# Second attention of a two-layer kernel: who splits, copies and divides the small rows between the big matmuls

## The reference, cut to what matters

```
x_norm = _rms_norm(x, g)
q = (x_norm @ w_q) ... * rf          # 16 heads of width 8
k = (x_norm @ w_k) ... * rf          # 4 heads
v = x_norm @ w_v
qkt  = einsum('brkqa,bkca->brkqc', q5, k) / sqrt(128)
attn = softmax(qkt, axis=-1)         # exp(s - rowmax(s)) / sum
s    = einsum('brkqc,bkca->brkqa', attn, v)
o    = s @ w_o
return s + o
```

## Time and profile before

| what | value |
|---|---|
| span of the profiled execution | 1651.9 us |
| second attention in it | about 520 to 1450 us |
| one batch of it (o in the middle) | 53.40 us |
| busy: PE matmuls / PE weight loads | 1455.9 (88%) / 716.9 (43%) us |
| busy: DVE / ACT / POOL | 1180.7 (71%) / 946.4 (57%) / 833.9 (50%) us |
| largest groups | `row_max` L1592 649.8 us on DVE, `exps` L1496 567.1 us on ACT, `scores` L1798 347.7 us on PE |

### The profile page before, as it was taken

How to read it: one execution, slowest core, us unless ns; L and a number is a source line. 1 busy time by engine, 2 the same in 40 slices (tenths; PEclk the granted TensorE clock), 3 DMA queues, 4 the chain that set the end, 5 groups by cost and what they waited for, 6 DMA issues and landing times. The chain is left out here.

```text
span 1651.9 us, 30013 instructions
## 1 busy us (share of the span) xinstructions
PE 1455.9 (88%) x9488; PEld 716.9 (43%) x9488; DVE 1180.7 (71%) x3123; ACT 946.4 (57%) x1805; POOL 833.9 (50%) x941
## 2 busy tenths in 40 slices
PE   3999999969993279999999999999999999849996
PEld 1444444469993123333333333333333332239996
DVE  3688777833334568899889998899989998514443
ACT  2565556524441147777777778777777777612221
POOL 4688888743003463556555655556565620114443
PEclk9999999979997569999999999999999999969998
DMA  1111211289995111122112221122212210347771
GB/s 38 46 56 54 64 56 49 80 242 298 304 296 145 57 56 46 56 77 73 55 55 65 78 61 54 57 75 73 59 55 62 70 51 13 108 155 239 236 241 58
DMA packets 144965, 165.76 MB, mean 100 GB/s; under 512 B 29073, under 2 KB 115217, under 8 KB 142649
## 3 DMA queue, kind: packets, MB, share of 16 engines
q1 hardware_dynamic: 92377, 74.76, 15.2%
q10 hardware_dynamic: 38608, 58.62, 11.6%
q0 software_dynamic: 13824, 30.47, 6.0%
HBM read 111.93 MB, written 51.30 MB: 99 GB/s over the span
## 5 line engine op out<-in xcount | busy, mean ns | idle before, releaser
L1592 DVE TENSOR_REDUCE c_mx<-c_ps_mx 128x1 f32<-128x512 f32 x1024 | 649.8, 683 | 89.6 <-PE c_ps_mx L1828 82.1
L1496 ACT ACTIVATE c_pt<-c_ps_e 128x512 f32<-128x512 f32 x1024 | 567.1, 601 | 189.9 <-PE c_ps_e L1798 176.3
L1798 PE MATMUL c_ps_e<-c_qst,c_kex 74*128 74x512 bf16 (+1 forms) x1024 | 347.7, 388 | 3.5 <-ACT c_pt L1496 1.9
L1811 PE MATMUL c_ps_v<-c_pt,c_vp 128*32 128x512 f32 x2048 | 274.5, 608 | 1.1 <-ACT c_pt L1496 0.7
L1333 POOL DMA_INDIRECT c_gy<-ys,mt x128 | 124.2, 970 | 276.5 <-PE c_ps_v L1811 129.9
L1828 PE MATMUL c_ps_mx<-c_kex,c_qst 64*128 64x512 bf16 x1024 | 204.6, 396 | 57.9 <-DVE c_mx L1592 40.9
L1828 PEld LDWEIGHTS c_ps_mx<-c_kex,c_qst 64*128 64x128 bf16 x1024 | 49.3, 93 | 367.8 <-DVE c_mx L1592 345.3
L998 PE MATMUL f_ps_h<-f_xT,f_w 128*128 128x256 f32 x800 | 197.0, 386 | 0.2 <-DVE f_xT L1064 0.2
L558 ACT ACTIVATE a_pt<-a_ps_s,temp 128x1024 f32<-128x1024 f32 (+3 forms) x128 | 113.1, 884 | 91.3 <-PE a_ps_s L652 86.3
L499 POOL DMA_INDIRECT xs<-a_xn,a_meta x128 | 135.6, 1059 | 38.1 <-issue 35.3
L998 PEld LDWEIGHTS f_ps_h<-f_xT,f_w 128*128 128x128 f32 x800 | 145.4, 194 | 15.9 <-issue 0.6
(11 more groups left out here) (225 smaller groups left out, 1895.0 us busy)
## 6 DMA issues: line engine op xcount, KB each, us to landing
f_w<-in_we ACTq DMA_DIRECT2D x80, 321.0 KB, 4.4
f_w<-in_we ACTq DMA_DIRECT2D x37, 576.0 KB, 4.5
c_qst<-qparts SPq DMA_DIRECT2D x75, 192.0 KB
f_x<-rows SPq DMA_DIRECT2D x40, 257.0 KB, 3.9
f_x<-xs SPq DMA_DIRECT2D x80, 128.0 KB, 4.4
ys<-f_y ACTq DMA_DIRECT2D x80, 128.0 KB, 4.3
qparts<-c_qp SPq DMA_DIRECT2D x16, 384.0 KB, 2.5
x<-in_x SPq DMA_DIRECT2D x16, 256.0 KB, 3.0
```

The costliest lines, as they stand in the source:

```text
L1496: nc.scalar.activation(pt[:, s % 4, hl, :], ps_e[:, e_bank(64 * b + n)], ACT.Exp, scale=QSCALE).then_inc(exp_done, 1)
L1592: nc.vector.tensor_reduce(mx[:, g % 2, col:col + 1], ps_mx[:, m_bank(64 * b + 2 * m + par)], AX, ALU.max).then_inc(mx_done, 1)
L1798: nc.tensor.matmul(ps_e[:, e_bank(64 * b + n)], kex[rows, p, k_head(hl), kt * P:(kt + 1) * P], qst[rows, p, q_head(g, hl), :], start=True, ...
L1811: last = nc.tensor.matmul(ps_v[32 * hl:32 * (hl + 1), :], vp[:, p, kt, hl, :], pt[:, s % 4, hl, :], start=kt == 0, stop=kt == NT - 1)
```

## The change

**Shift rows.** Before, PE transposed the 16 columns of maxima (float32), and DVE negated them and split them into two bfloat16 parts with two instructions out of PSUM. Now POOL splits the columns in SBUF (`split`: a cast to bfloat16, a wait for it, and a subtraction, 128x16 each, into `c_mxp`), PE turns both parts with one bfloat16 matmul (32 rows), and ACT negates and copies them to `c_shb`. SP's four DMAs stay; only their source's layout is new. PE's `max_columns` waits for `split_ready` and no longer for `mx_done`.

**Result rows.** Before, DVE took the reciprocal of the sums and multiplied, out of PSUM, four times a batch. Now ACT copies the 36 used columns of each of 4 blocks (`token_copy`, to `c_raw`) four times a batch, DVE takes one reciprocal of all 64 sums (`inverses`), and POOL multiplies once (`normalise`, 128x512). `s_rows` waits for POOL (`all_ready`).

**Places.** The small blocks are in other steps. PE: `s_rows` 2 to 3, `s_project` 3 to 4, `max_columns` of group 2 from 4 to 5, `token_rows` of group 0 from 5 to 6, `x_rows` from the middle of 7 to the end of 7, and the first `project` from the end of 7 to the middle of 8. `output` moves from step 4 to 5 on DVE; `xT_copy` and the first `prj_copy` from step 7 to 8 on ACT. On POOL the scatters carry the steps 6 to 9 instead of 5 to 8.

```diff
@@ POOL
+                def normalise(i, o):
+                    pool.wait_ge(rcp_ready, b + 1)
+                    pool.wait_ge(sT_ps, b)
+                    nc.gpsimd.tensor_tensor(sall[...], raw[...][:, :, 0:DH1], rcp[...].to_broadcast([P, NT * H1, DH1]),
+                                            ALU.mult).then_inc(all_ready, 1)
+                def split(i, o, g):
+                    pool.wait_ge(mx_done, 16 * (4 * b + g + 1) + 2)
+                    if not (isinstance(b, int) and 4 * b + g < 2):
+                        pool.wait_ge(mt_ps, 4 * b + g - 1)
+                    nc.gpsimd.tensor_copy(mxp[:, g % 2, 0], mx[:, g % 2]).then_inc(split_steps, 1)
+                    pool.wait_ge(split_steps, 4 * b + g + 1)
+                    nc.gpsimd.tensor_tensor(mxp[:, g % 2, 1], mx[:, g % 2], mxp[:, g % 2, 0], ALU.subtract).then_inc(split_ready, 1)
                 def body(i, o):
+                    split(i, o, 1)
                     if nxt2:
                         combine(ln, i, o + 2)
                     if nxt:
                         v_rows(i, o + 1)
+                    if prev:
+                        normalise(i, o - 1)
                     keep_xn(i, o)
                     if nxt2:
                         norms(ln, i, o + 2)
+                    split(i, o, 2)
+                    if nxt2:
                         normal_rows(i, o + 2)
                     if prev:
-                        for t in range(NT):
-                            scatter(i, o - 1, t, 5 + t)
+                        for t in range(3):
+                            scatter(i, o - 1, t, 6 + t)
+                    split(i, o, 3)
+                    if prev:
+                        scatter(i, o - 1, 3, 9)
...
                         gather(i, o + 3, (1,), 11)
                         gather(i, o + 3, (2,), 12)
+                    if nxt:
+                        split(i, o + 1, 0)
                     if nxt2:
                         k_parts(pc, i, o + 2)
@@ ACT
                     for s in range(16):
                         exps(i, o, s, 0)
-                        if s == 7 and nxt2:
+                        if s == 2 and prev:
+                            token_copy(i, o - 1, 3)
+                        if s in (7, 11, 15):
+                            token_copy(i, o, s // 4 - 1)
+                        if s in (1, 6, 9):
+                            shifts(i, o, s // 4 + 1)
+                        if s == 13 and nxt:
+                            shifts(i, o + 1, 0)
+                        if s == 8 and nxt2:
                             xT_copy(i, o + 2)
...
-                        if s == 2 and prev:
+                        if s == 3 and prev:
                             sT_copy(i, o - 1)
-                        if s == 7 and nxt2:
+                        if s == 8 and nxt2:
                             prj_copy(i, o + 2, 0)
@@ DVE
-                        if s in (1, 5, 9):
-                            shifts(i, o, s // 4 + 1)
-                        if s == 13 and nxt:
-                            shifts(i, o + 1, 0)
-                        if s == 1 and prev:
-                            normalise(i, o - 1, 3)
+                        if s == 2 and prev:
+                            inverses(i, o - 1)
-                        if s in (5, 10, 14):
-                            normalise(i, o, s // 5 - 1 if s < 14 else 2)
@@ PE
-                    pe.wait_ge(mx_done, 16 * (4 * b + g + 1) + 2)
-                    nc.tensor.transpose(ps_j[:, 0:P], mx[:, g % 2, :], k.ident[:]).then_inc(mt_ps, 1)
+                    pe.wait_ge(split_ready, 4 * b + g + 1)
+                    nc.tensor.matmul(ps_j[0:2 * NT * HL, 0:P], mxp[:, g % 2].rearrange("p n c -> p (n c)"), k.ident_b[:],
+                                     start=True, stop=True).then_inc(mt_ps, 1)
...
-                        if s == 7 and nxt2:
-                            free = x_rows(free, i, o + 2)
+                        if s == 8 and nxt2:
+                            free = project(free, i, o + 2, 0)
...
-                        if s in (0, 4, 8):
+                        if s in (0, 5, 8):
                             free = max_columns(free, i, o, s // 4 + 1)
...
-                        if s in (5, 10, 14):
-                            free = token_rows(free, i, o, s // 5 - 1 if s < 14 else 2)
+                        if s in (6, 10, 14):
+                            free = token_rows(free, i, o, s // 4 - 1)
                         if s == 7 and nxt2:
-                            free = project(free, i, o + 2, 0)
+                            free = x_rows(free, i, o + 2)
```

More of the change, by code:

```diff
@@ L1476, in _ @@
                 normal_rows(0, 1)
+                split(0, 0, 0)
                 pool.wait_ge(const_in, 48)
@@ L1502, in ov_copy, with token_copy, shifts @@
                     nc.scalar.activation(ov[:], ps_v[:], ACT.Copy).then_inc(ov_sb, 1)
+                def token_copy(i, o, g):
+                    b, h, p = batch(i, o)
+                    act.wait_ge(ot_ps, 4 * b + g + 1)
+                    if g == 0:
+                        act.wait_ge(all_ready, b)
+                    nc.scalar.activation(raw[:, :, g], ps_j[:].rearrange("p (t h c) -> p t h c", t=NT, h=HL)[:, :, :, 0:DH1 + 1],
+                                         ACT.Copy).then_inc(ot_sb, 1)
+                def shifts(i, o, g):
+                    b, h, p = batch(i, o)
+                    act.wait_ge(mt_ps, 4 * b + g + 1)
+                    if not (isinstance(b, int) and 4 * b + g < 2):
+                        act.wait_ge(sh_in[g % 2], 64 * (2 * b + g // 2))
+                    nc.scalar.activation(shb[:, g % 2, :], ps_j[0:2 * NT * HL, 0:P], ACT.Copy, scale=-1.0).then_inc(sh_ready, 1)
                 def xT_copy(i, o):
@@ L1572, in _ @@
                     xT_copy(0, o)
+                    if o == 1:
+                        shifts(0, 0, 0)
                     prj_copy(0, o, 0)
@@ L1696, in body @@
                         more = s + AHEAD < 16 or nxt
-                        if s == 4 and prev:
+                        if s == 5 and prev:
                             output(i, o - 1)
```

58 lines of the change are left out of this document (25 added, 33 removed).

## The result

The changed kernel takes 1770.06 us (median of 4 runs, 1765.64 to 1777.77) against 1650.94 for the kernel before (1650.28 to 1651.6): a ratio of 1.0724, 95% interval 1.0696 to 1.0752. It is slower, as forecast, but by 119 us and not by 76: the time lies 2 us above the upper end of the range. The prediction was worked out on the span of the profiled execution, and by spans the change costs 115.6 us (1767.5 for 1651.9); that execution's own time, 1769.18, stands 1.7 over its span.

The account below looks back on a forecast made before the run. The prediction took PE to set the pace, with small margin at the end places; its terms (-1.5 + 37 + 16 + 14 + 3 + 3.5 + 1.5 + 1.5 = 75) on the span of 1651.9 gave 1727 us, range 1690 to 1768.

Parts of the forecast that it names:

- Steps 7 and 8: Small blocks moved in steps 7 and 8 make PE wait for ACT's copies: 2.7 us in each of 14 batches, +37 us.
- the split behind the gather of step 12: POOL's split queued behind its gather DMA in step 12 delays PE's pair by 1.2 us in 13 batches, +16 us.
- the one at the batch's start: POOL's split behind three gathers of step 15 delays PE's pair after step 0 by 1.05 us, x13, +14 us.
- the other split of step 8: POOL's group 3 split behind the scatter of step 8, costing only in the last two batches, which don't project: +3 us.
- DVE's relief: Shift work and dividing taken off DVE, one reciprocal added: gain of 0.1 us a batch (bounds 0 and 2.2), -1.5 us.
- The first batch: PE waits for group 1 columns, which POOL splits only behind the low parts: +3.5 us (1 to 7).
- The end, put at 3: Uncovered copy and semaphores at the very end, +1.5 us; ACT's extra copies in the last half batch and start, +1.5.
- The clock falls too: Rival: PE's repeated stalls also lower its clock, 2.5 us a batch x14 = +35, giving 1762 us; chance 0.2.
- DVE was the bound: Rival: DVE bounds the kernel, so its relief gains up to 2.2 us a batch, giving 1619 us; chance 0.05.
- Only the ACT stalls bite: Rival: POOL runs its DMAs earlier than placed, so the split terms 16 + 14 + 3 go, giving 1694 us; chance 0.12.

## Why the prediction was too low

*What bounds the kernel.* Right in what mattered: PE's small blocks have little margin, and the time went into them. The room that DVE gets is real and worth little. With all blocks in time, and the statistics moved besides, the 15 batches are 6.1 us shorter: 0.4 a batch, 0.3 in the steady ones, for 4 us less work; the prediction took 0.1 and bounded it by 2.2. The rule of the Trainium skill that it weighed (Perfetto Trace Analysis, Identifying the Most-Contended Engine: relieve the engine of the highest occupancy first) would have given 1592. By the runs, relieving that engine brought 6 to 7 us in the batches where it did best, and these were given back in the first batch.

*The terms.* Steps 7 and 8 came as computed, 0.2 us longer; the split behind the gather of step 12 and the one at the batch's start within 0.1; the other split of step 8, covered in the changed kernel, showed its size when the cover was taken away. Together the stalls are 5.4 a batch (58.25 - 52.83) for 4.8 predicted. Most of the missing 0.6 is the 0.2 of steps 7 and 8 and "DVE's relief", entered as a gain of 0.1 from B of step 1 to A of step 5: it is a loss of 0.2 (12.24 us for 12.01), because the reciprocal took 0.54 for the 0.3 estimated and stands next to the statistics, so that A to B of step 3 is 2.51 and not 2.10. The first batch, up to the first `s_rows`, lost 10.85 where its terms (3.5 and the other places once) give 8.4; a fall of the clock is 1.5 of that. The end, put at 3, cost nothing: the last batch is 1.6 us longer (41.42 for 39.84), and that is the fall at 1533 us, for in the kernel with the places changed, which has no fall there, it takes 39.84 too. All stalls: 77.5 for 75.

*The step that failed* is the choice between the cases. The forecast let the clock stand, and the rival "The clock falls too", 1762, had a chance of 0.2 because "the longest stall is no more than half of the time around it". That argument was drawn from a single row of layer 0, and the runs refute it: behind stalls of 1.50 and 1.81 us the clock came down 22 times in 12 batches. The trace of before already spoke against it. At the row that it took (where "a second" should read a microsecond) PE had stood for 1.08 us, less than the stalls that the prediction computed, and the clock was at half from 124 us on:

```profile
124.40 2.08 PE L675 MATMUL a_ps_t<-wo,a_attnT 128*128 128x128 f32 x8 [1.08 <-DVE a_attnT L422]
```

The rival's size was nearly right: +35 computed, 38 measured. With it the sum is 75 + 35 = 110 on the span; 2.5 of the 5.6 missing are the stalls' and 3 the clock's, and 1.7 more stand between span and time. The range ended 6 us above the rival's time, which left no room for these.

*That the clock took the rest* is shown by the run with the projection's copy put first: 7 us of stall less and 33 us of time less, at a mean clock of 0.99 for 0.94 between 800 and 1400 us. What brings a fall is settled only in part. Stalls of 0.94, 1.32, 1.27 and 1.50 a batch gave two falls in 600 us; 1.50, 1.29 and 1.27, in the kernel with the places changed, gave ten, one of them twice as long; and with one stall taken out of four, batches with none, one and two falls follow each other. No sum over the stalls of a batch orders these runs. What the traces show besides is that the falls keep a time of their own. In the changed kernel 21 times running the next one starts 30.72 us after the last, though the batches vary from 61.31 to 61.69 (the stretches of 3.4 us are falls; the granted clock is again the last but two):

```profile
812.72:816.12 3.40, 3.40 (x14) 0.44 (x12) 1.29 (x2) 1.73 (x4) 0.03 (x1) 0.50 0.01 2
816.14:843.43 27.29, 23.94 (x152) 7.70 (x156) 21.43 (x42) 20.71 (x43) 16.94 (x22) 1.00 0.18 54
843.44:846.84 3.40, 3.07 (x15) 1.11 (x8) 1.80 (x3) 1.23 (x3) 3.24 (x3) 0.50 0.01 2
846.86:874.15 27.29, 22.97 (x139) 7.55 (x140) 20.94 (x52) 18.62 (x38) 12.75 (x21) 1.00 0.22 69
874.16:877.56 3.40, 3.40 (x14) 0.43 (x12) 1.29 (x2) 1.66 (x4) 0.14 (x1) 0.50 0.01 2
```

In the kernel with the splits ahead of the DMAs most of them start 58.02 or 58.03 us apart. So a stall does not start a fall by its length alone; it also counts when it comes. The changed kernel's stalls of 1.50 us that were followed by a fall ended 1.6 to 1.8 us ahead of it, each time. Its batches with two falls take 61.4 us in the mean, almost twice 30.72, so that each batch's stalls meet the same moments again; in batches of 57.77, with the copy first, the same stalls drift past them. That is read from the traces and not tested: no run moved a stall in time and left the rest alone. If it is right, the 26 us that the clock gave back for that copy are in part luck.

*The rivals.* "DVE was the bound" did not come, nor did it when everything else was mended. "Only the ACT stalls bite" did not come, since GpSimd's DMAs ran where they were placed.

*A better kernel.* The changed kernel with five things moved reaches 1649.5, 0.14% under the kernel before; the kernel before with one of these five reaches 1649.6, 0.16% under it. The change is worth nothing measurable here, once its waits are repaired.

## What to carry to other kernels

Before work is moved off the fullest engine, look at what stands ahead of it in the queue that it moves to: here one DMA issue of 0.96 us ahead of two operations of 0.2 us held up PE, and so did one copy on ACT. Stalls can be added up from the trace of before, block by block, and held within 0.15 us here. But when a change puts repeated stalls of 1 to 2 us into a stage that had none, do not treat falls of the clock as a tail: they were a third of the loss here. Their number can't be had from the stalls' lengths (from 2 to 20 in 600 us for much the same stalls), so give the sum without them and the sum with one behind each of the longer stalls, and let the range hold both. Then look in the trace of before for the shortest stall with a fall behind it.

## What the runs showed of the hardware

- A fall of TensorE's granted clock to 1.2 GHz lasted some 3.4 us in a stage that was at 2.4 GHz otherwise, and cost 1.55 us of time, a little less than half of it.
- It followed stalls of PE of 1.27 to 1.81 us, but not each of them. Falls started 30.72 us apart 21 times running, whatever the batches did. Which stall they followed changed from kernel to kernel; the spans of two executions of one kernel differed by 11 us at mean clocks of 0.943 and 0.946.
- A matmul record that a trace lacks makes the next wait look longer: 2.13 us for 1.81, 1.65 for 1.32, 1.61 for 1.29. The weight load's record shows where it was.
- DVE's reciprocal took 0.54 us for 64 elements a partition and 0.25 for 16 in the kernel before (half of the instructions of the second of the earlier trace rows): some 6 ns more for each element.
- GpSimd's two operations on 128x16 took 0.20 and 0.22 us, as near to its 128x4 operations as assumed.
